# Attention: heads stacked in pairs on 64-row tiles, the row maxima subtracted by products of their own, splits and normalisation moved to GpSimd

## What is computed

```python
x = x + attention(layernorm(x))       # 16 heads of 16 columns
x = x + ffn(layernorm(x))             # blockwise FP4 quantised linears

# attention
x_h = x.reshape(b, t, h, d).transpose(0, 2, 1, 3)
xw  = einsum('bhtd,hde->bhte', x_h, w_att_val)
att = softmax(einsum('bhte,bhse->bhts', xw, x_h) / sqrt(d))
vx  = (x @ wv_w.T + wv_b) split into heads
o   = einsum('bhts,bhsd->bhtd', att, vx) joined again
return o @ out_w.T + out_b
```

## Time and profile before

| what | value |
|---|---|
| median of 3 runs | 1644.62 us (1644.61 to 1647.51) |
| profiled execution, span | 1643.6 us |
| attention block, first maxima product to last projection | about 65.9 to 1076 us |
| TensorE busy | 1573.4 us (96%), 7850 matmul records |
| VectorE busy | 1397.6 us (85%) |
| ScalarE busy | 842.4 us (51%) |
| GpSimd busy | 328.4 us (20%) |

### The profile page before, as it was taken

How to read it: one execution, slowest core, us unless ns; L and a number is a source line. 1 busy time by engine, 2 the same in 40 slices (tenths; PEclk the granted TensorE clock), 3 DMA queues, 4 the chain that set the end, 5 groups by cost and what they waited for, 6 DMA issues and landing times. The chain is left out here.

```text
span 1643.6 us, 30806 instructions
## 1 busy us (share of the span) xinstructions
PE 1573.4 (96%) x7850; PEld 990.7 (60%) x7850; DVE 1397.6 (85%) x2849; ACT 842.4 (51%) x1714; POOL 328.4 (20%) x448
## 2 busy tenths in 40 slices
PE   3499999999999999999999999869999999999998
PEld 3255655655655655655655655446666666666666
DVE  7588888888888888888888887269999999999996
ACT  2166566566566566566566566623333333333332
POOL 2601101101101101101101101023334433344332
PEclk8589999999999999999999999979999999999999
DMA  4735455455455455455455455000000000000000
GB/s 162 154 81 131 93 117 130 92 117 130 92 117 130 92 117 128 93 117 127 94 117 127 94 105 133 3 0 17 16 13 16 16 16 16 13 16 16 16 16 20
DMA packets 67937, 127.28 MB, mean 77 GB/s; under 512 B 22592, under 2 KB 42176, under 8 KB 59456
## 3 DMA queue, kind: packets, MB, share of 16 engines
q1 hardware_dynamic: 60128, 119.53, 33.3%
q10 hardware_dynamic: 7776, 7.36, 2.1%
HBM read 81.67 MB, written 45.15 MB: 77 GB/s over the span
## 5 line engine op out<-in xcount | busy, mean ns | idle before, releaser
L938 DVE TENSOR_REDUCE neg_max<-max_bank 128x1 f32<-128x512 f32 x1024 | 660.4, 683 | 159.0 <-PE max_bank L751 158.1
L880 ACT ACTIVATE probs<-scores 128x512 f32<-128x512 f32 x1024 | 551.2, 599 | 340.8 <-PE scores L759 340.7
L759 PE MATMUL scores<-q_stack,x_stack 98*128 98x512 f32 x1024 | 448.3, 440 | 2.5 <-ACT probs L880 2.0
L751 PE MATMUL max_bank<-x_stack,q_stack 96*128 96x512 f32 x1024 | 413.7, 410 | 16.5 <-DMA x_stack<-x_split 15.1
L759 PEld LDWEIGHTS scores<-q_stack,x_stack 98*128 98x128 f32 x1024 | 193.6, 190 | 245.7 <-ACT probs L880 208.4
L1304 PE MATMUL gu_bank<-splits,f_x_T 128*128 128x352 f32 x1024 | 315.7, 462 | 2.1 <-ACT f_x_T L1282 2.1
L770 PE MATMUL pv<-probs,v_quad 128*32 128x512 f32 x2048 | 272.7, 605 | 0.0
L1304 PEld LDWEIGHTS gu_bank<-splits,f_x_T 128*128 128x128 f32 x1024 | 190.6, 191 | 98.4 <-ACT f_x_T L1282 2.7
L751 PEld LDWEIGHTS max_bank<-x_stack,q_stack 96*128 96x128 f32 x1024 | 198.8, 194 | 53.4 <-issue 15.9
L1322 PE MATMUL y_bank<-splits,h_T 128*128 128x256 f32 x640 | 148.9, 380 | 1.1 <-ACT h_T L1262 1.1
L1262 ACT ACTIVATE h_T<-h_bank 128x512 f32<-128x512 f32 (+1 forms) x128 | 49.0, 434 | 194.5 <-PE h_bank L1314 194.5
(11 more groups left out here) (123 smaller groups left out, 1741.6 us busy)
## 6 DMA issues: line engine op xcount, KB each, us to landing
q_stack<-q_split SPq DMA_DIRECT2D x256, 128.0 KB, 4.0
x_stack<-x_split SPq DMA_DIRECT2D x128, 256.0 KB, 6.0
x_split<-splits SPq DMA_DIRECT2D x64, 256.0 KB, 2.2
q_split<-splits SPq DMA_DIRECT2D x64, 256.0 KB, 2.6
out_dram<-x_all SPq DMA_DIRECT2D x64, 128.0 KB, 1.7
x_all<-in_L_attn_x_dram ACTq DMA_DIRECT2D x14, 512.0 KB, 6.0
max_rows<-max_turned SPq DMA_DIRECT2D x256, 4.0 KB, 4.2
splits<-gate_up_kept SPq DMA_DIRECT2D x1, 1408.0 KB, 5.8
```

The costliest lines, as they stand in the source:

```text
L751: pe.matmul(max_bank[bank][:, :], q_stack[g][0:KM, h, s * P:(s + 1) * P], x_stack[g][0:KM, h, :], start=True, stop=True).then_inc(m_ready, 1)
L759: pe.matmul(scores[bank][:, :], x_stack[g][0:KS, h, j * P:(j + 1) * P], q_stack[g][0:KS, h, :], start=True, stop=True).then_inc(s_ready, 1)
L880: act.activation(probs[j % 2][:, h, :], scores[bank_of(g, QUAD * j + h)[0]][:, :], ACT.Exp).then_inc(p_ready, 1)
L938: dve.tensor_reduce(neg_max[g % 2][:, TT * h + s:TT * h + s + 1], max_bank[bank_of(g, TT * h + s)[0]][:, :], AX.X, ALU.max, negate=True).t ...
```

## The change

- Two heads share a stack's 128 rows: head pair member m has rows 64m to 64m + 63 (`row_tile`), the free dimension holds two heads (PAIRS) instead of four. `KM` is 64; no zero rows remain. The products of a pair stand one after the other on the two row tiles.
- The maxima are no longer rows of q_stack. They are loaded to `max_stack`, rows 64m and 64m + 1, the other rows zero, and a second product with `max_ones` adds them to the bank. So a pair has two products on the data and two on the maxima. A pair waits for both of its banks at once.
- In a step: first pair of scores, pair of max products, W of the step before, second pair of scores, pair of max products, then the work of `IN_STEP`. The heads' order in a bank sequence is that of `head_of`.
- ScalarE copies x and q from misc into `raw` in SBUF (`keep`), after the step's exponentials; GpSimd makes high (times one) and low (`split`). The products of q and v wait for x_low, the stores for x_low or q_low.
- GpSimd normalises (`normalize`): two instructions per 128 rows (subtract the mean, multiply) instead of one on VectorE.
- `load_stacks` issues twelve DMAs of half the size instead of six; `load_maxima` loads with two instead of one.
- The memsets before the loop change with the stacks (`set_up`); VectorE has none now.

```diff
+PAIRS = 2
+ROWS = 2
 BLK = 16
 VW = 32
-KM = 96
-KS = KM + 2
+KM = 4 * D
...
-    q_stack = [sb(f"q_stack{g}", [P, QUAD, T], F32R) for g in range(QUADS)]
-    x_stack = [sb(f"x_stack{g}", [P, QUAD, T], F32R) for g in range(QUADS)]
+    q_stack = [sb(f"q_stack{g}", [P, PAIRS, T], F32R) for g in range(QUADS)]
+    x_stack = [sb(f"x_stack{g}", [P, PAIRS, T], F32R) for g in range(QUADS)]
+    max_stack = [sb(f"max_stack{u}", [P, PAIRS, T], F32R) for u in range(2)]
+    max_ones = sb("max_ones", [P, 1, P], F32R)
+    x_mid = sb("x_mid", [P, E])
+    one = sb("one", [P, 1])
+    raw = [sb(f"raw_{n}", [P, T]) for n in "xq"]
...
+    def head_of(place):
+
+        return 2 * (place % ROWS) + place // ROWS
+
+    def row_tile(tile, m):
+
+        return tile[KM * m:KM * m + KM, :, :]
...
+            def set_up():
+                n = 0
+                for u in range(2):
+                    n = fill(n, max_stack[u][:, :, :].bitcast(F32), 0.0)
+                n = fill(n, one[:, :], 1.0)
+                n = fill(n, max_ones[:, :, :].bitcast(F32), 0.0)
+                for m in range(ROWS):
+                    n = fill(n, max_ones[KM * m:KM * m + 2, :, :].bitcast(F32), 1.0)
...
+            def split(kind, b):
+
+                a = int(kind[1])
+                at, high, low, high_done, low_done, stored = (
+                    (raw[0], xh, xl, xh_done, x_low, x_stored) if kind[0] == "x" else
+                    (raw[1], qh, ql, qh_done, q_low, q_stored))
+                pool.wait_ge(misc_used, use(kind, b) + 1)
+                pool.wait_ge(stored[a], 32 * (b + 1))
+                pool.tensor_tensor(high[:, a, :], at[:, :], one[:, :].broadcast_to([P, T]), ALU.mult).then_inc(high_done, 1)
+                pool.wait_ge(high_done, HALVES * (b + 1) + a + 1)
+                pool.tensor_tensor(low[:, a, :], at[:, :], high[:, a, :].bitcast(F32), ALU.subtract)\
+                    .then_inc(low_done, 1)
...
+            def normalize(d):
+                pool.wait_ge(rstd_done, d + 1)
+                pool.wait_ge(misc_ready, use("x1", d - 2) + 1)
+                for s in range(TT):
+                    if s > 0:
+                        pool.wait_ge(xn_done, TT * d + s)
+                    pool.tensor_tensor(x_mid[:, :], x_all[:, bass.ds(d * TT + s, 1), :].rearrange("p o e -> p (o e)"),
+                                       mean_var[:, s, 0:1].broadcast_to([P, E]), ALU.subtract).then_inc(x_centred, 1)
+                    pool.wait_ge(x_centred, TT * (d - 2) + s + 1)
+                    pool.tensor_tensor(xn[:, s, :].rearrange("p (a d h) -> p a d h", d=D, h=HH),
+                                       x_mid[:, :].rearrange("p (a h d) -> p a d h", d=D, h=HH),
+                                       rstd[:, s:s + 1].unsqueeze(2).unsqueeze(3).broadcast_to([P, HALVES, D, HH]),
+                                       ALU.mult).then_inc(xn_done, 1)
+
             def batch(b):
-                for g in range(QUADS):
-                    quad(b, g, isinstance(b, int) and b == 0)
+                first = isinstance(b, int) and b == 0
+                for g in range(3):
+                    quad(b, g, first)
+                if prepared(b + 1):
+                    split("x0", b)
+                quad(b, 3, first)
+                if prepared(b + 1):
+                    split("q0", b)
                 if prepared(b + 2):
                     deviation(b + 2)
-
-            n = set_up(POOL_SETS, 0)
-            pool.wait_ge(pool_set, n)
+                if prepared(b + 1):
+                    split("x1", b)
+                    split("q1", b)
+                if prepared(b + 2):
+                    normalize(b + 2)
...
-                for k in range(4):
-                    src = q_split[bass.ds(b, 1), a, k // 2, :, h0:h0 + QUAD, :]
-                    sp.dma_start(q_stack[g][D * k:D * k + D, :, :].bitcast(F32), src.rearrange("o d h t -> (o d) h t"))\
-                      .then_inc(stack_loaded[g], 16)
-                for k in range(2):
-                    src = x_split[bass.ds(b, 1), a, :, :, h0:h0 + QUAD, :]
-                    sp.dma_start(x_stack[g][2 * D * k:2 * D * k + 2 * D, :, :].bitcast(F32),
-                                 src.rearrange("o l d h t -> (o l d) h t")).then_inc(stack_loaded[g], 16)
+                for m in range(ROWS):
+                    h = h0 + PAIRS * m
+                    for k in range(4):
+                        src = q_split[bass.ds(b, 1), a, k // 2, :, h:h + PAIRS, :]
+                        sp.dma_start(row_tile(q_stack[g], m)[D * k:D * k + D, :, :].bitcast(F32),
+                                     src.rearrange("o d h t -> (o d) h t")).then_inc(stack_loaded[g], 16)
+                    for k in range(2):
+                        src = x_split[bass.ds(b, 1), a, :, :, h:h + PAIRS, :]
+                        sp.dma_start(row_tile(x_stack[g], m)[2 * D * k:2 * D * k + 2 * D, :, :].bitcast(F32),
+                                     src.rearrange("o l d h t -> (o l d) h t")).then_inc(stack_loaded[g], 16)
...
-                sp.dma_start(q_stack[g][96:KS, :, :].bitcast(F32),
-                             max_rows[bass.ds(i, 1)].rearrange("o (l h s) r t -> (o l) h (s r t)", l=2, h=QUAD))\
-                  .then_inc(max_loaded[g], 16)
+                if isinstance(i, int) and i < 2:
+                    sp.wait_ge(pool_set, ZEROED)
+                else:
+                    sp.wait_ge(s_ready, QUAD * TT * (i - 1))
+                rows = max_rows[bass.ds(i, 1)].rearrange("o (l h s) r t -> (o l) h (s r t)", l=2, h=QUAD)
+                for m in range(ROWS):
+                    sp.dma_start(max_stack[g % 2][KM * m:KM * m + 2, :, :].bitcast(F32),
+                                 rows[:, PAIRS * m:PAIRS * m + PAIRS, :]).then_inc(max_loaded[g], 16)
...
-            def max_scores(i, b, g, h, tiles, start):
-
-                if h == 0 and tiles[0] == 0:
+            def max_scores(i, b, g, n, start):
+
+                p, s = divmod(n, TT)
+                if n == 0:
                     pe.wait_ge(stack_loaded[g], STACK * (b + 1))
-                for s in tiles:
-                    bank, back = bank_of(g, TT * h + s)
-                    if not (start and TT * h + s < 3):
-                        pe.wait_ge(m_used, QUAD * TT * i + TT * h + s - back + 1)
-                    pe.matmul(max_bank[bank][:, :], q_stack[g][0:KM, h, s * P:(s + 1) * P],
-                              x_stack[g][0:KM, h, :], start=True, stop=True).then_inc(m_ready, 1)
-
-            def key_scores(i, g, j, h, start):
-
-                bank, back = bank_of(g, QUAD * j + h)
-                if not (start and j == 0 and h < 3):
-                    pe.wait_ge(p_ready, QUAD * (TT * i + j) + h - back + 1)
-                pe.matmul(scores[bank][:, :], x_stack[g][0:KS, h, j * P:(j + 1) * P],
-                          q_stack[g][0:KS, h, :], start=True, stop=True).then_inc(s_ready, 1)
+                banks = [bank_of(g, ROWS * n + m) for m in range(ROWS)]
+                free = [ROWS * n + m - banks[m][1] + 1 for m in range(ROWS) if not (start and ROWS * n + m < 3)]
+                if free:
+                    pe.wait_ge(m_used, QUAD * TT * i + max(free))
+                for m in range(ROWS):
+                    pe.matmul(max_bank[banks[m][0]][:, :], row_tile(q_stack[g], m)[:, p, s * P:(s + 1) * P],
+                              row_tile(x_stack[g], m)[:, p, :], start=True, stop=True).then_inc(m_ready, 1)
+
+            def key_scores(i, g, j, p, start):
+
+                at = [QUAD * j + ROWS * p + m for m in range(ROWS)]
+                banks = [bank_of(g, k) for k in at]
+                free = [k - bank[1] + 1 for k, bank in zip(at, banks) if not (start and k < 3)]
+                if free:
+                    pe.wait_ge(p_ready, QUAD * TT * i + max(free))
+                for m in range(ROWS):
+                    pe.matmul(scores[banks[m][0]][:, :], row_tile(x_stack[g], m)[:, p, j * P:(j + 1) * P],
+                              row_tile(q_stack[g], m)[:, p, :], start=True, stop=False)
+                for m in range(ROWS):
+                    pe.matmul(scores[banks[m][0]][:, :], row_tile(max_ones, m)[:, 0, :],
+                              row_tile(max_stack[g % 2], m)[:, p, :], start=False, stop=True).then_inc(s_ready, 1)
...
+                    if half == 0:
+                        pe.wait_ge(x_low, HALVES * (c - 1) + a + 1)
...
+                    for p in range(PAIRS):
+                        key_scores(i, g, j, p, start)
+                        if ahead:
+                            max_scores(i + 2, ab, ag, PAIRS * j + p, False)
+                        if p == 0 and j > 0:
+                            weigh_values(i, b, g, j - 1, start)
+                        elif p == 0 and not start:
+                            weigh_values(i - 1, b - (g == 0), (g - 1) % QUADS, TT - 1, False)
+                    if stands(kind, b):
                         for half in range(2):
```

(20 more changed lines are left out.)

## The result

The changed kernel takes 1656.2 us (1653.1 to 1658.5, four runs) against 1644.6 us; the ratio is 1.007, with an interval of 1.0051 to 1.0089. It is slower, where I had forecast faster. The profiled execution took 1653.1 us with a span of 1651.3 us, 7.7 us longer than the span before.

The account below looks back on a forecast made before the run. TensorE's own order of work was taken as the bound, 61.6 us per batch. Span 1643.6 - 18 (batches) + 4 + 4 (both ends of the attention) = 1633.6, rounded up to 1636 us; range 1603 to 1700.

Parts of the forecast that it names:

- the changes of form: TensorE switching between 128-row extra work and row pairs in a step: taken as 0.24 us for each extra.
- the wait for x_low: TensorE's q products waiting for the low part of x that GpSimd makes: 0.35 us, twice per batch (0 to 0.95).
- start, to the first S: First 32 max products, before the first products that feed the exponentials, paced by VectorE: +4 us (0 to 5).
- the 15.5 batches: Attention loop in steady form, a batch being 16 steps: 1.2 us better per batch, -18 us in all.
- last two quads, to the turning of the last rows: End of the attention, without max products: a step goes from 2.61 to 3.08 us, eight times 0.47, +4 us.
- hand-over to the FFN: Passage from attention to the second block: no change forecast, 0 us; the FFN itself was called untouched.
- One slot for a pair: Two products on two row tiles take TensorE one 512-column product's time, loads side by side: 0.47 us less per step.
- SyncE's added stack loads: Rival: twelve stack loads per quad instead of six delay the maxima's load in the same queue; up to 1670; chance 0.14.
- 1735: Estimate in us within the rival that pairs do not fully overlap (chance 0.13): 4/3.07 on each slot.
- the gate: Chain from one score pair's load to the next, through the first exponential: 0.54 + 0.23 + 0.60 + 0.05 = 1.42 us.
- the plain step: Loop step without extra work: 1.42 + 1.89 = 3.31 us against 3.06, 0.25 worse, twice per batch.
- The rival of cheap changes of form: Switching array form is cheap and x_low is in time: 2.1 us per batch more saved, 1603 us; chance 0.15.

## Why the prediction was wrong

The sign was wrong by two terms of the batch, both priced too low: the changes of form, by 1.0 us, and the wait for x_low, by 0.6. The ledger of the span, forecast and measured:

| part | forecast | measured |
|---|---|---|
| start, to the first S | +4 | +3.7 (90.59 against 86.91) |
| the 15.5 batches | -18 | +3.8 |
| last two quads, to the turning of the last rows | +4 | +4.3 |
| hand-over to the FFN | 0 | -4.0 |
| FFN | 0 | -0.1 |
| span (parts rounded) | -10 | +7.7 |

The last two quads are counted from the first S of the last quad but one (1039.84 before, 1047.32 after) to the turning of their last rows (1063.30 and 1075.10).

**Right: the pairs.** One slot for a pair, no wait of S for max_stack in the loop and with it no effect of SyncE's added stack loads, M pairs at the start 67.70 to 69.27 = 1.57 apart with VectorE idle for 0.29, steps of the last quads 3.07. The start:

```profile
67.70 0.80 PE L804 MATMUL max_bank<-x_stack,q_stack 64*128 64x512 f32 x2 [0.78 <-DVE neg_max L1002]
68.53 1.29 DVE L1002 TENSOR_REDUCE neg_max<-max_bank 128x1 f32<-128x512 f32 x2 [0.29 <-PE max_bank L804]
...
69.27 0.80 PE L804 MATMUL max_bank<-x_stack,q_stack 64*128 64x512 f32 x2 [0.78 <-DVE neg_max L1002]
```

The speedup in the Trainium skill, "TensorE: Matmul & The Clock Gate", Part 3, from which I had estimated 1735, doesn't carry to two tiles of 64 rows: four tiles of 32 rows gave 3.07 there, two give 2 here (0.47 against 0.24).

**Right: the gate** of 1.42, to the hundredth, and with it the plain step of 3.31. It is the price of taking banks by pairs from three. It makes the plain steps 0.25 longer than before and so explains 0.5 us of a batch, not more. By kind of step a batch changed thus: plain +0.5, transposes 8 x -0.13 = -1.0, q +1.1, v -0.2, projection -0.1. The slots saved in the other steps, 0.47 each, went for the most part into the two terms below.

**Wrong in size: the change of form.** I took 0.24 per extra. Measured, by TensorE's own work in the step less the slots that I had counted: transposes 1.48 - 0.80 - 0.35 = 0.33, q products 3.91 - 1.89 - 0.80 - 0.92 = 0.30, v 0.29, projection 0.36 to 0.43. The kernel before with one product on 64 rows shows the same price, 0.36 to 0.41, by itself. This lifts the transposing steps over the gate, 3.37 instead of 3.31, eight times: 0.5 us per batch; with q, v and the projection 1.0. In all the changes of form take 8 x 0.33 + 2 x 0.30 + 2 x 0.29 + 0.79 = 4.6 us of a batch, out of the 7.5 that the slots save. The Trainium skill, "TensorEngine Tiling (Array Packing)", Key Properties, has the rule that a change of tiling mode drains the engine; the trace agrees (0.33 and 0.43 from start to start at the two changes, 0.23 without one), and the rows here give the price. The rival of cheap changes of form had the wrong sign.

**Wrong in size: the wait for x_low.** I forecast 0.35, twice. TensorE came to the q products when I said: the last M pair starts at 527.45, and where nothing is waited for the q product follows 0.33 later, so 4.28 after the pair (forecast 4.31); raw_x began at 525.23 - 523.50 = 1.73 (1.75). But x_low was ready to be used at 528.46 - 523.50 = 4.96 instead of 4.66. Half of that is the second GpSimd operation: 1.27 with two full operands, where I had 1.08 from rows that read one full operand; the first, times a broadcast column, took 1.04. The other half is the handing over between engines, 0.17, 0.08 and 0.06, where I had 0.05 each. By starts the wait is 4.96 - 4.28 = 0.68 (the 0.62 in the record counts from the modelled end of M), and the step lost 0.70 (4.61 against 3.91), the other one 0.58. I had named the range, 0 to 0.95, and 1.38 as the upper bound of the operation, but took the middle.

Together, per batch: changes of form 1.0 (0.5 from transposes, 0.3 from the projection, 0.1 each from q and v), wait 0.6 (0.70 + 0.58 - 2 x 0.35). They make 1.6. My own terms add up to 60.3 before I rounded the gain to 1.2, and 61.83 - 60.3 = 1.5 was measured. Over 15.5 batches, measured against the 60.4 of the forecast, that is 22 us, which turns -18 into +4, as measured. Neither term decides the sign alone. Without the excess of the wait (15.5 x 0.6 = 9 us) the batches would come to -5, and the two ends take 8; the run without the splits on GpSimd agrees, with 1646.05. Without the excess of the changes of form (15.5 x 1.0 = 16 us) they would come to -12, and -4 would be left. The forecast of -10 needed both.

In the first quads, where more steps have no extra, these take 3.30 us against 3.05 to 3.08 before; in the total this is small.

**Missed: the hand-over.** The last projections ran at the high clock level, where before they were at the low one:

```profile
1079.22 1.99 PE L888 MATMUL misc<-out_T,o_T 128*128 128x256 f32 x8 [0.69 <-ACT o_T L950]
1082.00 1.99 PE L888 MATMUL misc<-out_T,o_T 128*128 128x256 f32 x8 [0.78 <-DVE x_all L1073]
```

Before:

```profile
1067.88 3.78 PE L824 MATMUL misc<-out_T,o_T 128*128 128x256 f32 x8 [0.69 <-ACT o_T L889]
1072.44 3.73 PE L824 MATMUL misc<-out_T,o_T 128*128 128x256 f32 x8 [0.78 <-DVE x_all L1029]
```

The difference is 3.5 of the 4.0 us given back, and it agrees with the higher digit in the clock row. It is no merit of the change: the same pair of records took 3.78 and 3.78 with q a step later, 1.99 and 1.99 with the moves to GpSimd alone, and 3.47 and 1.99 with the row pairs alone. The idle times just ahead are 0.69 and 0.78 or 0.79 in all of them; what decides where the clock falls is open.

**The median and the span.** The median rose by 11.6 us, the span of the profiled execution by 7.7. The mean granted clock, recorded for every run, goes with the difference: the changed kernel took 1653.1 and 1654.0 us at 0.977 and 0.976, and 1658.4 and 1658.5 at 0.973. The kernel before, in 17 runs taken beside later experiments, took 1641.6 to 1644.5 at 0.976 and 0.977, and 1645.9 to 1648.8 at 0.973 and 0.974; its profiled execution had 0.974. At like clock the change costs 10 to 11 us, which is what the ledger gives without the clock of the hand-over (7.7 + 3.5 = 11.2). That the lower clock of the unprofiled runs lay in the hand-over, too, isn't shown.

## What to carry to other kernels

Packing two products on row tiles halves their slots, but it also makes their banks come free in pairs: before it is counted as a gain, work out the chain from one pair to the next, and put other work into the steps where that chain ends last. Price every change between products of different form with a run of its own: here they took 4.6 us of a batch, the wait for x_low 1.3. The pairs alone were worth 0.5 us of a batch and nothing in the total, until v's products filled the idle steps and the banks' irregular places were moved; then the kernel was 0.7% faster than the one before. That the kernel before would gain nothing from the same two moves was not tested; it has no gate that its plain steps idle at. An operation that is moved to a slower engine (the low part took 0.68 us on VectorE and 1.28 on GpSimd) costs nothing only where its reader stands far enough behind; count each semaphore of that chain, and when the reader can be moved by one step, move it. Where banks rotate with an irregular place, put that place into the step with the most slack, for each kind of bank by itself.

## What the runs showed of the hardware

- Two products of 512 columns on two 64-row tiles take one slot, 0.24 us, and their loads fall together (0.19 us for both); on one tile they take 0.47.
- Going from a product on 98 or 128 rows to one on 64 and back costs 0.36 to 0.41 us together, though the columns are the same.
- The clock level of the few products of the hand-over differs between the profiled executions, by up to 3.6 us of span, and runs of one kernel at a mean granted clock of 0.973 took some 4 us more than at 0.976 and 0.977 (1658.4 and 1658.5 against 1653.1 and 1654.0). A span or a median of few runs can't tell such a difference from one in the loop; the distance of the batches can, and so can a comparison of runs at like clock.
- GpSimd on 128 x 512: 1.04 us times a broadcast column, 1.28 us (60 records) for a subtraction of two full tiles.
